# Transformer block with an 8-expert layer on 8 cores: per-tile waits in the dense feed-forward stage, and four-slot loads in the last stage

## What is computed

```python
def layer_norm(x, gamma, beta): ...
def attn(xn):                       # linear attention, 16 heads of 64
    ...                             # Q, K = elu(.) + 1; out = Q (K^T V) Z; @ Wo + bo
    x = layer_norm(xn + linear_attention(xn), g1, beta1)
    y = relu(x @ W1 + b1) @ W2 + b2          # 1024 -> 4096 -> 1024
    return layer_norm(x + y, g2, beta2)
def ffn(xn):                        # 8 experts, each token in two of them
    h = mod(int32(xn[:, 0] + xn[:, 1]), 8); sel = [h, (h + 1) % 8]
    for e in range(8):
        w = any(sel == e) / 2
        acc += w * (relu(xn @ W1[e] + b1[e]) @ W2[e] + b2[e])
    return acc
xn = layernorm(x)
return x + attn(xn) + ffn(xn)
```

## Time and profile before

| | |
|---|---|
| time, median of 2 runs | 5845.3 us (5844.91 to 5845.69) |
| the profiled execution | 5846.2 us, span of its slowest core 5844.7 us |
| spans of the 8 cores | 5836.5 to 5844.7 us |
| mean granted TensorE clock | 0.906 to 0.908 on all cores |
| TensorE busy with matmuls | 4869.6 us (83%) |
| VectorE, ScalarE, GpSimd busy | 1698.2, 1139.6, 344.5 us |

### The profile page before, as it was taken

One profiled execution on the slowest core, in us unless ns is written; L12 is line 12 of the kernel. 1 busy time (PEld: TensorE's weight loads), 2 busy tenths in 40 slices (PEclk: granted clock), 3 DMA queues, 4 the chain that ended last, 5 costly groups with the idle time before them and its releaser, 6 DMA issues.

```text
span 5844.7 us, 55999 instructions; the slowest of 8 cores (5836.5 to 5844.7 us)
## 1 busy us (share of the span) xinstructions
PE 4869.6 (83%) x21665; PEld 2133.2 (36%) x21665; DVE 1698.2 (29%) x3207; ACT 1139.6 (19%) x2205; POOL 344.5 (6%) x661
## 2 busy tenths in 40 slices
PE   4777499999999999999999999999986433777752
PEld 2333144444444444444444444444432210333311
DVE  2444222222222222222322222222224224111154
ACT  3444211111111111111111111111102123011120
POOL 1000000000000000000000000000000000000000
PEclk8777799999999999999999999999987665999965
DMA  3000022222222222222222222222212110111103
GB/s 59 29 29 29 14 40 38 35 38 38 37 37 38 37 37 38 38 37 39 38 35 38 38 35 38 38 35 38 40 22 35 43 38 8 26 29 22 27 6 115
DMA packets 105684, 209.48 MB, mean 36 GB/s; under 512 B 12960, under 2 KB 13232, under 8 KB 105424
## 3 DMA queue, kind: packets, MB, share of 16 engines
q0 software_dynamic: 91056, 163.84, 18.3%
q1 hardware_dynamic: 14368, 42.06, 2.1%
HBM read 361.06 MB, written 8.39 MB: 63 GB/s over the span
## 4 chain that ended last, share of the span: by engine, by line
PE 78%; DVE 8%; ACT 6%; DMA 4%; issue 3%; POOL 0%; DVEq 0%; ACTq 0%; SPq 0%; POOLq 0%
PE ps L726 31%; PE ps L764 31%; PE ps L1134 4%; PE ps L1113 4%; PE ps L475 3%; DMA xt_b<-xs 1%; ACT h_b L1123 1%; DMA xtm_b<-xs 1%; PE ps L770 1%; PE ps L455 1%; DVE x_sb L1151 1%; PE ps L957 1%; DVE ln_t L1073 1%; DVE acc L788 1%; DVE scol L414 1%
## 5 line engine op out<-in xcount | busy, mean ns | idle before, releaser
L726 PE MATMUL ps<-xnbf,w1s 128*128 128x512 bf16 x8192 | 1825.6, 381 | 53.6 <-DVE wb L711 32.3
L726 PEld LDWEIGHTS ps<-xnbf,w1s 128*128 128x128 bf16 x8192 | 799.3, 98 | 1046.6 <-issue 105.6
L764 PE MATMUL ps<-h_hi,w2s 128*128 128x512 bf16 x4096 | 923.6, 384 | 22.5 <-DVE acc L788 22.5
L764 PE MATMUL ps<-h_lo,w2s 128*128 128x512 bf16 x4096 | 904.9, 379 | 0.0
L788 DVE TENSOR_TENSOR acc<-acc,ps 128x512 f32<-128x512 f32 x992 | 614.9, 681 | 836.4 <-PE ps L764 533.9
L736 ACT ACTIVATE h_lo<-ps,eb_sb 128x512 bf16<-128x512 f32 x512 | 309.8, 688 | 1542.2 <-PE ps L726 1542.2
L764 PEld LDWEIGHTS ps<-h_hi,w2s 128*128 128x128 bf16 x4096 | 404.8, 99 | 521.7 <-issue 51.4
L736 ACT ACTIVATE h_hi<-ps,eb_sb 128x512 bf16<-128x512 f32 x512 | 309.8, 688 | 1461.7 <-PE ps L726 1461.7
L764 PEld LDWEIGHTS ps<-h_lo,w2s 128*128 128x128 bf16 x4096 | 400.8, 98 | 483.2
L744 DVE TENSOR_TENSOR h_lo<-h_lo,wb 128x512 bf16<-128x512 bf16 x512 | 183.2, 420 | 948.5 <-ACT h_lo L736 948.5
L744 DVE TENSOR_TENSOR h_hi<-h_hi,wb 128x512 bf16<-128x512 bf16 x512 | 183.1, 419 | 898.2 <-ACT h_hi L736 898.2
(11 more groups left out here) (178 smaller groups left out, 2280.4 us busy)
## 6 DMA issues: line engine op xcount, KB each, us to landing
w1s<-ew_pk POOLq DMA_DIRECT2D x256, 256.0 KB, 3.5
w2s<-ew_pk POOLq DMA_DIRECT2D x256, 256.0 KB, 3.5
xtm_a<-xs SPq DMA_DIRECT2D x32, 512.0 KB, 3.2
xt_b<-xs SPq DMA_DIRECT2D x32, 256.0 KB, 2.7
w1s<-w_pk POOLq DMA_DIRECT2D x32, 256.0 KB, 3.6
w2s<-w_pk POOLq DMA_DIRECT2D x32, 256.0 KB, 3.5
xtm_b<-xs SPq DMA_DIRECT2D x16, 512.0 KB, 3.9
out<-otm_b SPq DMA_DIRECT2D x16, 512.0 KB, 2.9
```

The source lines that it names most:

```text
L726: self.em("T", lambda t, k=k, tt=tt, slot=slot: t.matmul(ps[tt][:], self.w1t(slot, k), self.xnbf[:, k * TOWN + tt * 512:k * TOWN + (tt + 1 ...
L764: self.em("T", lambda t, j=j, tt=tt, slot=slot, hreg=hreg, lp=last_plain: t.matmul(ps[4 + tt][:], self.w2t(slot, j), hreg[:, j * TOWN + tt ...
```

## The change

`emit_b2` makes the token tile the outer loop of a block and the weight chunk the inner one. Each tile has its own semaphore steps: TensorE waits before a tile's eight matmuls for the eviction of that bank alone, ScalarE and VectorE wait for one tile's matmuls at a time and step the semaphore for each tile. The wait that keeps ScalarE from overwriting `h_b2` while Y blocks still read it (`regEv`) becomes a wait of TensorE at the first H block of a group (`mmY_tt`). The refill of a weight slot goes by the last tile of a block, as before.

`emit_b4` has four slots each for loading and for storing, its loads are issued by GpSimd and its stores by SP, and it borrows idle semaphores for the new slots.

```diff
-        self.xtm_b4 = sb("xtm_b4", [128, 2 * D], F32, TR, 196608)
-        self.otm_b4 = sb("otm_b4", [128, 2 * D], F32, TR + 8192, 196608)
+        self.xtm_b4 = sb("xtm_b4", [128, 4 * D], F32, TR, 196608)
+        self.otm_b4 = sb("otm_b4", [128, 4 * D], F32, TR + 16384, 196608)
...
-                self.wait("T", self.s_sc, hEv_prev)
-                for k in range(KC):
-                    for tt in range(4):
+                mmH_tt = [0] * 4
+                for tt in range(4):
+                    self.wait("T", self.s_sc, hprev_tt[tt])
+                    if i == 0:
+                        self.wait("T", self.s_mm, mmY_tt[tt])
+                    for k in range(KC):
                         self.em("T", lambda t, k=k, tt=tt, slot=slot: t.matmul(
...
-                mmH = self.inc("T", self.s_mm, 1)
-                self.w1_ev.append((self.s_mm, mmH))
-                self.wait("S", self.s_mm, mmH)
-                if regEv:
-                    self.wait("S", self.s_mm, regEv)
+                    mmH_tt[tt] = self.inc("T", self.s_mm, 1)
+                self.w1_ev.append((self.s_mm, mmH_tt[3]))
                 for tt in range(4):
+                    self.wait("S", self.s_mm, mmH_tt[tt])
                     self.em("S", lambda s, tt=tt, i=i, n=n: s.activation(
...
-                hEv_prev = self.inc("S", self.s_sc, 1)
+                    hprev_tt[tt] = self.inc("S", self.s_sc, 1)
+                hlast_tt = list(hprev_tt)
             for dout in range(KC):
...
-                self.wait("T", self.s_sc, hEv_prev)
-                self.wait("T", self.s_ve, yEv_prev)
-                for j in range(GH):
-                    for tt in range(4):
+                mmYc = [0] * 4
+                for tt in range(4):
+                    self.wait("T", self.s_sc, hlast_tt[tt])
+                    self.wait("T", self.s_ve, yadd_tt[tt])
+                    for j in range(GH):
...
-                self.wait("V", self.s_mm, mmY)
-                self.wait("V", self.s_ve, yEv_prev)
                 for tt in range(4):
...
+                    self.wait("V", self.s_mm, mmYc[tt])
+                    self.wait("V", self.s_ve, yadd_tt[tt])
...
-                yEv_prev = self.inc("V", self.s_ve, 1)
+                    yadd_tt[tt] = self.inc("V", self.s_ve, 1)
 
     def emit_b4(self):
...
+        ldsem = [self.s_eb[0], self.s_eb[1], self.s_w1[0], self.s_w1[1]]
+        stsem = [self.s_st[0], self.s_st[1], self.s_lx[0], self.s_lx[1]]
...
+            sl = j % 4
...
-            if j >= 2:
-                self.wait("Y", self.s_ve, evAdd[j - 2])
-            lxv = self.dma("Y", xt, self.xs[j * 128:(j + 1) * 128, :], self.s_lx[par])
+            if j >= 4:
+                self.wait("G", self.s_ve, evAdd[j - 4])
+            lxv[j] = self.dma("G", xt, self.xs[j * 128:(j + 1) * 128, :], ldsem[sl])
...
-            self.wait("V", self.s_lx[par], lxv)
+            self.wait("V", ldsem[sl], lxv[j])
+            if j >= 4:
+                self.wait("V", stsem[sl], stv[j - 4])
...
             self.wait("Y", self.s_ve, evAdd[j])
-            self.dma("Y", self.out[j * 128:(j + 1) * 128, :], ot, self.s_st[par])
+            stv[j] = self.dma("Y", self.out[j * 128:(j + 1) * 128, :], ot, stsem[sl])
```

More of the change, by code:

```diff
@@ L1101, in emit_b2 @@
         ps = self.ps
-        hEv_prev = 0
-        yEv_prev = 0
-        regEv = 0
+        hprev_tt = [0] * 4
+        hlast_tt = [0] * 4
+        mmY_tt = [0] * 4
+        yadd_tt = [0] * 4
         for gg in range(NGRP):
@@ L1137, in emit_b2 @@
                             start=(j == 0), stop=(j == GH - 1)))
-                mmY = self.inc("T", self.s_mm, 1)
-                self.w2_ev.append((self.s_mm, mmY))
+                    mmYc[tt] = self.inc("T", self.s_mm, 1)
+                self.w2_ev.append((self.s_mm, mmYc[3]))
                 if dout == KC - 1:
-                    regEv = mmY
-                self.wait("V", self.s_mm, mmY)
-                self.wait("V", self.s_ve, yEv_prev)
+                    mmY_tt = mmYc
                 for tt in range(4):
                     xsl = self.x1_sb[:, dout * TOWN + tt * 512:dout * TOWN + (tt + 1) * 512]
+                    self.wait("V", self.s_mm, mmYc[tt])
+                    self.wait("V", self.s_ve, yadd_tt[tt])
                     if gg == 0:
@@ L1156, in emit_b4 @@
         evAdd = {}
+        ldsem = [self.s_eb[0], self.s_eb[1], self.s_w1[0], self.s_w1[1]]
+        stsem = [self.s_st[0], self.s_st[1], self.s_lx[0], self.s_lx[1]]
+        lxv = {}
+        stv = {}
         for j in range(NGOWN):
+            sl = j % 4
             par = j % 2
-            xt = self.xtm_b4[:, par * D:(par + 1) * D]
-            ot = self.otm_b4[:, par * D:(par + 1) * D]
-            if j >= 2:
-                self.wait("Y", self.s_ve, evAdd[j - 2])
-            lxv = self.dma("Y", xt, self.xs[j * 128:(j + 1) * 128, :], self.s_lx[par])
+            xt = self.xtm_b4[:, sl * D:(sl + 1) * D]
+            ot = self.otm_b4[:, sl * D:(sl + 1) * D]
+            if j >= 4:
+                self.wait("G", self.s_ve, evAdd[j - 4])
+            lxv[j] = self.dma("G", xt, self.xs[j * 128:(j + 1) * 128, :], ldsem[sl])
             pbase = 0 if par == 0 else 2
-            if j >= 2:
-                self.wait("V", self.s_st[par], (j // 2) * 16)
             self.wait("T", self.s_ve, evAdd.get(j - 2, 0))
@@ L1180, in emit_b4 @@
             self.wait("Y", self.s_ve, evAdd[j])
-            self.dma("Y", self.out[j * 128:(j + 1) * 128, :], ot, self.s_st[par])
-        self.wait("Y", self.s_st[0], self.s_st[0].n)
-        self.wait("Y", self.s_st[1], self.s_st[1].n)
+            stv[j] = self.dma("Y", self.out[j * 128:(j + 1) * 128, :], ot, stsem[sl])
+        for s in stsem:
+            self.wait("Y", s, s.n)
+        for s in ldsem:
+            self.wait("Y", s, s.n)
         if self.s_sd.n:
```

## The result

| | before | changed |
|---|---|---|
| times, without executions at a lower clock | 5844.7 to 5847.8 us | 5597.2 to 5599.9 us |
| ratio to before, 95% interval | | 0.9577 (0.9561 to 0.9594) |
| the profiled execution, span of its slowest core | 5846.2, 5844.7 | 5600.4, 5598.9 |
| `emit_b2`, first weight load to the next stage's first instruction | 657.6 | 448.8 |
| `emit_b4`, first load's issue to the end | 97.3 | 53.2 |

The account below looks back on a forecast made before the run. TensorE's waits for PSUM evictions were taken to bound emit_b2, and load latency emit_b4. 5846.2 - 208.8 (emit_b2) - 45 (emit_b4) = 5592.4, with the median 0.9 lower, said as 5592 us; range 5580 to 5638.

Parts of the forecast that it names:

- the first term of the sum: Whole kernel: starting time of 5846.2 us, the profiled execution before, from which both gains are subtracted.
- the likeliest case: Whole kernel: both gains arrive as priced, 5592 us, own range 5580 to 5606, chance 0.78.
- No engine late for its new wait: emit_b2: each per-tile wait finds its work done, covered by 4.4 us to spare; priced at nothing.
- The weight loads: emit_b2: refills issue and land in 4.1 us against blocks of 6.91, longest 0.1 late once; priced at nothing.
- The clock term of 30.4 us: emit_b2: 19 slow blocks besides the first vanish once the gaps go, 30.4 us of the 208.8 gain.
- Rival B: emit_b2: eight matmuls in a row into one bank pay up to 0.163 us each, 292 us, 5884; chance 0.04.
- Rivals A and D: emit_b2: A, slow blocks stay without gaps, 5622 us, chance 0.07; D, dense matmuls lower the clock, 5639 to 6034, 0.03.
- Edit 2: emit_b4: four slots and loads on GpSimd's queue remove serial store issue and load flight, 97.3 to 52 us, gain 45.
- The DMA bound: emit_b4: DMA traffic is the next limit, 16.78 MB at 346 GB/s takes 48.5 us, 3.0 per step.
- slots don't bind: emit_b4: load, adds and refill take 6 us, even doubled by queueing 12 for four steps, 3.0 each.
- first data after 1.9 us: emit_b4: start term of its 52 us sum, the shortest latency drawn from the rows, about 1.9 us.
- Rival C: emit_b4: the four slots don't overlap, stage keeps 72 to 97 us, kernel taken as 5637; chance 0.07.

Follow-up runs that it names:

- edit 2 alone: Only the changed emit_b4 (four slots, loads on GpSimd) put in the kernel before; no ratio, cores 4 to 7 took 5796.1 to 5801.0 us.

## Why the prediction was right, and where it was not

**The step that failed.** 5592 us was forecast, with a range of 5580 to 5638, and the median over all 11 executions is 5733.0. The step is the first term of the sum, "5846.2 (profiled execution; span 5844.7 and 1.5 around it)". That is an execution with the full clock on both dies, and the sum only takes the two gains off it; it has no term for a die at a lower clock. In the execution with the median time cores 0 to 3 took 5584.9 to 5596.0 us at a mean clock of 0.913 to 0.914, and cores 4 to 7 took 5719.8 to 5731.5 at 0.885 to 0.889: 135 us more. 7 of the 11 executions had such a die. The kernel before has it too: 6 of its 10 took 6027.6 to 6713.9 us. What such a die does can be seen in the execution traced for edit 2 alone, on its core 0, in two stretches of the expert stage, columns as in the earlier trace rows:

```profile
2000.00:2100.00 100.00, 100.00 (x383) 41.43 (x381) 22.63 (x47) 14.54 (x24) 6.36 (x12) 0.81 0.20 32
3000.00:3100.00 100.00, 100.00 (x465) 45.34 (x464) 27.37 (x56) 19.15 (x32) 7.95 (x15) 1.00 0.25 38
```

TensorE is full in both, at a granted clock of 0.81 in one and of 1.00 in the other: 383 matmuls in place of 465. What sets this off, no run here shows.

**The size and the sum.** Without such a die the times are 5597 to 5600, inside both the stated range and the likeliest case's own, and 0.9577 of 5845.3 is 5598. The terms of the sum are checked on these.

**The missing 6 us.** Both gains were met: 208.8 forecast and 208.8 measured for `emit_b2`, 45 and 44.1 for `emit_b4`. Yet the span, 5598.9, is 7.1 us longer than 5844.7 - 208.8 - 44.1 = 5591.8. Of these 1.2 lie between the two stages (149.3 for 148.1), and 5.9 ahead of `emit_b2`: it starts at 4947.50 on the slowest core after, and at 4941.62 on the slowest before, which is another core. The sum lets everything outside the two stages stay as it was; that term was mis-sized. 2.7 of the 5.9 are there from the first Y block of the expert stage on (L764 starts at 764.7, before at 762.0), and still when `emit_b1` sends its first load (4526.10, before 4523.44). The other 3.2 come between there and `emit_b2`. `emit_b1`, which neither edit touches, loads 32 tiles one at a time and waits for each. On the slowest core after, the transposes' group reads

```profile
L936 PE MATMUL ps<-ident,xt_b 128*128 128x128 f32 x128 | 34.8, 428 | 123.6 <-DVE xt_b L928 123.6
```

and before

```profile
L936 PE MATMUL ps<-ident,xt_b 128*128 128x128 f32 x128 | 34.8, 428 | 119.0 <-DVE xt_b L928 119.0
```

These waits are 4.6 us longer, where the whole way from the first load to `emit_b2` is 3.2 longer. Among the cores of one execution the first matmul of `emit_b2` starts between 4939.0 and 4952.7 after (4940.0 to 4947.4 before), and the median landing of these loads lies between 2.5 and 2.8 us: which cores are slow there differs from one traced execution to the next. Why some loads land later was not tried and stays open. Holding the untouched stages fixed is good to about this much.

**No engine late for its new wait.** Right. In the changed `emit_b2` TensorE waits for no eviction at all. ScalarE's 128 evictions each wait for TensorE, as they should.

**The weight loads.** Right. They land in a median of 3.6 us, 7.7 at most for `w1s` (6.5 before), and TensorE waited for the very first one only.

**The clock term of 30.4 us.** Right, and now separated from the rest: the order alone leaves the 19 slow blocks, the waits alone remove them, and alternating banks remove them without the tile order. The reason given, that they come from the gaps, is borne out: with the gaps of 2.7 us they are there, and with waits of 0.3 us between H blocks in their place they are not. (The prediction puts them after every second or third gap; in the chain before they come one to six blocks apart, mostly three.)

**Rival B, one bank eight times in a row.** Excluded by its own run: 0.9997 of before, where it would have cost up to 292 us.

**Rivals A and D, the clock.** Excluded for the executions compared: the granted clock is 1.00 from 4960 to 5380. The current limit of the Trainium skill (TensorE: Matmul & The Clock Gate, section "Seeing it yourself") gave 5694; with all eight cores on dense matmuls the compared executions show 1.00. The dies at a lower clock do show that page's level, though: 13/16 is 0.8125, and the granted clock in the first stretch above is 0.81. It is 0.81 too in the changed `emit_b2` on core 0 of the execution traced for two slots:

```profile
5500.00:5600.00 100.00, 99.29 (x375) 41.41 (x382) 11.63 (x16) 22.00 (x32) 6.37 (x12) 0.81 0.20 32
```

So the prediction's "this trace disagrees" was read from an execution in which the level does not appear, and D's clock does come in others. It does not come from the missing gaps, as the expert stage, which nobody changed, has it too. That it is the limit which the page means is likely by its level and is not shown.

**Edit 2.** The DMA bound was the right next limit: 16.78 MB in 53.2 us, at share 0.92 and 312 GB/s mean. The term "slots don't bind" holds for four slots, but only just: flights grew to 9.8 us, so that load, adds and refill take 0.5 + 9.8 + 1.5 = 11.8 us, and the doubling allowed for was 12; with two slots the stage is 15 us longer. The sum's first data after 1.9 us and a transfer of 1.5 was too early: four loads set out together, and the first add starts 5.1 us after the first of them (5550.75 and 5545.66). Rival C is excluded at its price, 72 to 97 us for the stage, though loads and stores do slow each other down.

## What to carry to other kernels

When one engine fills all its PSUM banks and another must empty them before the next block, make the banks end apart (the tile outer, the contraction inner) and wait for each, or alternate two sets: either removes the wait whole, while waits for each bank with the old order gave half. Count the clock with it: the wait of 2.7 us at nearly every block cost 30 us more than the waits themselves. In a load, compute, store stage look first at what stands behind what in the issuing queue; once transfers filled the DMA engines (share 0.92), what still helped here was to move bytes to an idle stage. And before a forecast starts from one execution, look at how the others of the same kernel spread: two of them, 0.8 us apart, said nothing of the 6027.6 to 6713.9 us that 6 of the next 8 took.

## What the runs showed that I had not expected

Turns 1.5 us longer than a block, with three matmuls in the middle of the break, left the clock at 1.00 through the stage, where single waits of 2.7 us gave 0.94. A die's clock can be 0.81 for a part of the same stage and 1.00 for the rest, with TensorE equally full. And a load whose landing takes two and a half times as long (9.8 us for 3.9) went with a stage little over half as long: the flight of a single transfer is no measure of a stage in which several are under way.
